# A causal mask carried in unused contraction rows of q and k, in place of identity-triangle products

## The chip, the core and the metric

The kernel runs on one core of a Trainium2 chip. The metric is the device time of one execution in microseconds (us). TensorE (PE in the profile) multiplies, VectorE (DVE) and ScalarE (ACT) read its results, GpSimd (POOL) helps beside them, and every DMA is issued from SyncE's queue (SPq in the profile) and runs on the core's 16 DMA engines.

## What is computed

Sixteen independent batches of 256 tokens of width 128 pass through causal attention with 16 heads of width 8, a residual and a layer norm, then a product with int8-rounded operands, a residual and a second layer norm.

```python
qkv = encodings @ attn_w.T + attn_b            # 16 heads, head width 8
mask = jnp.arange(n)[:, None] <= jnp.arange(n)[None, :]
scores = jnp.einsum('bhki,bhqi->bhkq', k, q) / math.sqrt(HEAD)
scores = jnp.where(mask, scores, NEG_INF)      # key k counts for query q only if k <= q
probs = jax.nn.softmax(scores, axis=2)         # over the keys
combined = jnp.einsum('bhkq,bhkl->bhql', probs, v)
x = _layernorm(x + (combined @ out_w.T + out_b))
x = _layernorm(x + ffn(x))                     # ffn: both operands rounded to int8, product, rescaled
```

## The kernel before

**Scores.** Two heads make a pair (PAIRS = 8). For a pair, 48 contraction rows hold one head and 48 the other: q and k are each split in three bf16 parts, and six products of parts of eight values give 48 rows (ROWS). Rows 96 to 123 are zero, rows 124 to 127 (SHIFT_ROW to DEPTH) carry a shift of each query, its largest score taken off in two bf16 pieces, against ones in `k_stat`. A score tile has 2 x 64 keys (64 of each head, KB = 64) on the partitions and the queries from the first of those keys on as columns: 256, 192, 128 or 64 of them for the four blocks of keys. The triangle on the diagonal is masked by one more product, `identb` by `causal` (-1e30 above the diagonal), which is added to the first 64 columns of every head pair in the bank.

**Units.** The tiles are computed in 12 units for a batch (`UNITS`: first key, first pair, number n of pairs): n is 2 for the first two blocks of keys and 4 for the last two. Every batch goes through the units twice: `scores_for_max` writes to a ring of 3 PSUM banks (`dve_bank`), which DVE reduces to maxima (L642), and `scores_for_exp` to a ring of 4 banks (`act_bank`), which ACT exponentiates into `probs` (L481). The maxima of batch b run 10 units ahead of the exponentials of batch b - 1 or so (`LEAD`): in phase b the exponentials of batch b stand beside the last two units of the maxima of batch b + 1 and the first ten of batch b + 2.

**Phases.** The programs of all engines are a loop over phases b from -4 to 18, each of 12 steps u, one for each unit, with the other work hung in at a fixed step: PE does the products of probabilities and values (`pv`, L860), the projections `project_qk(b + 4)` (L881, at u = 6 and 7), `project_v`, `turn_maxima(b + 1)` (u = 4), the output projection and the feed-forward product of earlier batches. All engines run their own list in order and meet at semaphores.

**From a projection to the scores.** ACT copies q and k of batch b + 4 out of PSUM (L498, L499), POOL, DVE and POOL again split them in three parts (L419, L421, L656, L424). SyncE writes the parts to DRAM images (`write_image`, L302), waits until these have landed, and reads them back into `q_move` and `k_stat`, which form a ring of 4 slots (`read_image`, L315 and L316): four DMAs of 192 KB in pieces of 512 bytes. A phase of SyncE is this list, in this order:

```python
            def phase(b):
                write_image(b + 3, 1)
                load_x(b)
                read_image(b + 3)
                load_xt(b + 5)
                load_shift(b + 1)
                write_image(b + 4, 0)
                store(b - 3)

            phases(phase, {-3: first_rows_stand, -2: next_rows_stand, -1: last_rows_stand})
```

`load_shift(b + 1)` (L325) moves the shift made by DVE (L675) into rows 124 to 127 of `q_move`: two DMAs of 8 KB in pieces of 64 bytes. `scores_for_exp(b + 1, 0)`, the first step of phase b + 1 on PE, waits for them. The `..._rows_stand` functions run before the phases -3, -2 and -1: the second and third copy the ones rows into two slots of `k_stat` each (L337, two DMAs of 32 KB on 4 partitions). POOL sets the constants and clears the buffers before its own phases (L377 to L400).

Of the kernel before, what the change touches and what calls it, by code (L numbers as in the profile page):

```python
# [45 lines left out]
KB = 64  # L46
# [14 lines left out]
MASKED = -1e30  # L61
MAGIC = 12582912.0
# [57 lines left out]
def build_program(nc, x, xt, wqkv_t, bqkv, wo_t, bo, rhs_t, out):  # L120
    ctx = ExitStack()
    with ctx:
# [26 lines left out]
        causal = sb("causal", [128, KB], BF16)  # L149
# [14 lines left out]
        q_move = [sb(f"q_move{i}", [128, PAIRS, TOK], BF16) for i in range(QK_RING)]  # L164
# [42 lines left out]
        ones_loaded = sem("ones_loaded")  # L207
        x_loaded = [sem(f"x_loaded{i}") for i in range(RING)]
# [54 lines left out]
        POOL_FIRST = 14  # L263
        POOL_ROWS = POOL_FIRST + 2 * (QK_RING - 2)
# [6 lines left out]
        def _(sp):  # L271
# [21 lines left out]
            def write_image(b, half):  # L293
# [4 lines left out]
                if half == 0:  # L298
                    wait_ring(sp, qk_loaded, b - QK_RING, 4, 4)
# [5 lines left out]
            def read_image(b):  # L305
# [5 lines left out]
                for s in range(2):  # L311
# [3 lines left out]
                    sp.dma_start(q_move[slot][rows, :, :], q[s]).then_inc(qk_loaded[slot], 16)  # L315
                    sp.dma_start(k_stat[slot][rows, :, s, :], k[s]).then_inc(qk_loaded[slot], 16)  # L316

            def load_shift(b):
# [4 lines left out]
                for part in range(2):  # L323
                    row = SHIFT_ROW + 2 * part
                    sp.dma_start(q_move[b % QK_RING][row:row + 2, :, :].rearrange("s p (c q) -> s (p c) q", q=32),  # L325
                                 shift[:, part, :]).then_inc(shift_loaded, 16)

            def store(b):
# [3 lines left out]
                sp.dma_start(out[b].rearrange("(t p) d -> p t d", p=128), o[:, :, :]).then_inc(stored, 16)  # L332

# [6 lines left out]
            def first_rows_stand():  # L340
                sp.wait_ge(rows_set, 1)
                sp.wait_ge(pool_setup, 1)

            def next_rows_stand():

                sp.wait_ge(rows_set, 2)
                sp.wait_ge(pool_setup, POOL_FIRST)
                set_shift_rows((0, 1))

            def last_rows_stand():  # L350
                sp.wait_ge(pool_setup, POOL_ROWS)
                set_shift_rows(range(2, QK_RING))
# [15 lines left out]
        def _(pool):  # L368
# [8 lines left out]
            step(pool.memset(q_move[0][:, :, :].bitcast(F32), 0.0))  # L377
            step(pool.memset(ident[:, :], 0.0))
            step(pool.memset(identb[:, :], 0.0))
            step(pool.memset(causal[:, :], MASKED))  # L380
# [649 lines left out]
```

## Time and profile before

| | |
|---|---|
| three runs | 284.0, 283.8 and 280.09 us, median 283.8 |
| the profiled execution | 284.06 us, of which the span of its trace is 282.3 |
| busy, share of the span | PE 87%, DVE 69%, ACT 67%, POOL 43% |
| granted TensorE clock, mean | 0.95 |
| DMA | 32.77 MB, 116 GB/s over the span |

A busy share is an average over a start of some 44 us, twelve phases that repeat, four that thin out and a tail; PE's busy time also counts matmuls that wait in the array for one another. What a stage costs is read from the time between the same steps of two phases.

### The profile page before, as it was taken

What the parts mean: (1) busy time and instruction counts of PE and PEld (TensorE: products, weight loads), DVE (VectorE), ACT (ScalarE), POOL (GpSimd) and SP (SyncE); (2) the same over time, 40 slices, a digit from 0 to 9 for tenths busy, and PEclk for the clock granted to TensorE, in tenths of its full rate; (3) what the DMA queues carried; (4) which work ended last, traced back from release to release, by engine and by line L of the source; (5) the groups of instructions that cost most, each with busy time, mean ns of one, the idle gap of its engine ahead of it and who ended that gap; (6) DMA issues with size and microseconds to landing.
All of it is one profiled execution on the core that took longest, in us unless ns stands there. A gap on an engine that the chain in (4) does not pass through costs nothing.

```text
span 282.3 us, 8298 instructions
## 1 busy us (share of the span) xinstructions
PE 244.5 (87%) x3075; PEld 171.2 (61%) x3077; DVE 195.1 (69%) x545; ACT 188.1 (67%) x434; POOL 121.8 (43%) x236
## 2 busy tenths in 40 slices
PE   4179747999999999999999999999999999999420
PEld 2037525676767676767676767676767677565200
DVE  7927853576869696868686868686868797624331
ACT  4202033677687787878787878787878777798341
POOL 7930840041525454545453535353535141532542
PEclk9999985999999999999999999999999999999855
DMA  3385777337554765476547654757466410110001
GB/s 93 111 189 121 165 154 196 77 116 152 173 93 134 133 193 92 151 134 192 91 153 135 192 91 151 135 170 118 151 116 190 76 41 15 31 37 16 7 19 37
DMA packets 50887, 32.77 MB, mean 116 GB/s; under 512 B 7200, under 2 KB 50848, under 8 KB 50848
## 3 DMA queue, kind: packets, MB, share of 16 engines
q1 hardware_dynamic: 50848, 32.26, 47.2%
q8 instruction: 24, 0.39, 0.6%
q14 instruction: 15, 0.12, 0.2%
HBM read 17.17 MB, written 14.68 MB: 113 GB/s over the span
## 4 chain that ended last, share of the span: by engine, by line
PE 81%; DVE 7%; issue 4%; POOL 3%; ACT 3%; DMA 1%; ACTq 0%; SPq 0%; POOLq 0%; DVEq 0%
PE pv_bank L860 18%; PE dve_bank L823 17%; PE act_bank L823 13%; PE act_bank L881 6%; PE dve_bank L826 5%; PE act_bank L826 5%; PE act_bank L891 3%; PE dve_bank L905 3%; PE dve_bank L923 3%; PE pv_bank L960 3%; PE act_bank L914 1%; PE dve_bank L871 1%; PE dve_bank L942 1%; PE act_bank L933 1%; POOL rstd L444 1%
## 5 line engine op out<-in xcount | busy, mean ns | idle before, releaser
L642 DVE TRANSPOSE_TENSOR_REDUCE part_max<-dve_bank 128x16 f32<-128x512 f32 (+1 forms) x192 | 115.8, 615 | 42.7 <-PE dve_bank L826 40.6
L481 ACT ACTIVATE probs<-act_bank 128x512 f32<-128x512 f32 (+1 forms) x192 | 101.2, 530 | 38.0 <-PE act_bank L826 37.1
L823 PE MATMUL act_bank<-q_move,k_stat 128*128 128x128 bf16 (+3 forms) x512 | 68.2, 236 | 6.2 <-issue 6.2
L823 PE MATMUL dve_bank<-q_move,k_stat 124*128 124x128 bf16 (+3 forms) x512 | 71.1, 241 | 1.6 <-DMA k_stat<-imagek 1.3
L860 PE MATMUL pv_bank<-probs,v_stat 128*32 128x256 f32 (+3 forms) x1024 | 61.1, 311 | 0.0
L823 PEld LDWEIGHTS dve_bank<-q_move,k_stat 124*128 124x128 bf16 x512 | 40.3, 117 | 28.9 <-DVE part_max L642 7.5
L419 POOL TENSOR_TENSOR qk_rest<-qk_f,qk_parts 128x512 f32<-128x512 f32 x15 | 17.4, 1162 | 75.5 <-ACT qk_f L499 72.4
L823 PEld LDWEIGHTS act_bank<-q_move,k_stat 128*128 128x128 bf16 x512 | 42.0, 114 | 10.7 <-issue 8.2
L826 PE MATMUL dve_bank<-causal,identb 128*128 128x128 bf16 (+1 forms) x192 | 46.5, 242 | 0.0
L826 PE MATMUL act_bank<-causal,identb 128*128 128x128 bf16 (+1 forms) x192 | 46.0, 240 | 0.0
L498 ACT ACTIVATE qk_parts<-act_bank,bias 128x256 bf16<-128x256 f32 x32 | 21.0, 655 | 26.6 <-PE act_bank L881 24.6
L860 PEld LDWEIGHTS pv_bank<-probs,v_stat 128*32 128x32 f32 x1024 | 20.3, 108 | 19.4 <-issue 9.7
L442 POOL TENSOR_SCALAR rstd<-moments 128x2 f32<-128x2 f32 x32 | 6.1, 191 | 52.7 <-DVE moments L713 35.6
L881 PE MATMUL act_bank<-xt_in,wqkv 128*128 128x256 f32 x64 | 23.3, 455 | 4.2 <-DMA wqkv<-wqkv_dram 3.7
L444 POOL TENSOR_TENSOR rstd<-rstd,minus_half 128x2 f32<-128x2 f32 x32 | 22.4, 699 | 2.7
L424 POOL TENSOR_TENSOR qk_parts<-qk_rest,qk_parts 128x512 bf16<-128x512 f32 x15 | 17.4, 1162 | 10.3 <-DVE qk_parts L656 10.3
L513 ACT ACTIVATE v_stat<-act_bank 64x256 f32<-64x256 f32 x32 | 12.1, 378 | 13.6 <-POOL v_stat L408 7.6
L826 PEld LDWEIGHTS dve_bank<-causal,identb 128*128 128x128 bf16 x192 | 19.0, 99 | 0.3
L826 PEld LDWEIGHTS act_bank<-causal,identb 128*128 128x128 bf16 x192 | 19.1, 99 | 0.1
L499 ACT ACTIVATE qk_f<-act_bank,bias 128x256 f32<-128x256 f32 x32 | 19.1, 596 | 0.0
L881 PEld LDWEIGHTS act_bank<-xt_in,wqkv 128*128 128x128 f32 x64 | 11.0, 205 | 11.4 <-issue 6.0
L565 ACT ACTIVATE o<-r,rstd 128x128 f32<-128x128 f32 x32 | 14.1, 496 | 4.6 <-POOL rstd L448 4.6
(87 smaller groups left out, 319.1 us busy)
## 6 DMA issues: line engine op xcount, KB each, us to landing
imageq<-qk_parts SPq DMA_DIRECT2D x32, 192.0 KB, 2.1
imagek<-qk_parts SPq DMA_DIRECT2D x32, 192.0 KB, 2.1
q_move<-imageq SPq DMA_DIRECT2D x32, 192.0 KB, 3.7
k_stat<-imagek SPq DMA_DIRECT2D x32, 192.0 KB, 4.4
xt_in<-xt_dram SPq DMA_DIRECT2D x16, 128.0 KB, 4.6
x_in<-x_dram SPq DMA_DIRECT2D x16, 128.0 KB, 2.4
out_dram<-o SPq DMA_DIRECT2D x16, 128.0 KB, 2.0
q_move<-shift SPq DMA_DIRECT2D x32, 8.0 KB
```

The source lines that it names most:

```text
L419: pool.tensor_tensor(qk_rest[:, :, :], qk_f[:, :, :], first, ALU.subtract).then_inc(qk_split[1], 1)
L424: pool.tensor_tensor(third, qk_rest[:, :, :], second, ALU.subtract).then_inc(qk_split[1], 1)
L444: pool.tensor_tensor(t[:, 0, :], t[:, 0, :], minus_half[:, :], ALU.pow).then_inc(made[1], 1)
L481: act.activation(probs[u][:, 0:cols], act_bank[at % ACT_BANKS][:, 0:cols], ACT.Exp, scale=SCALE).then_inc(act_emptied, 1)
L498: act.activation(first, src, ACT.Identity, bias=bias[:, w:w + 1])
L499: act.activation(whole, src, ACT.Identity, bias=bias[:, w:w + 1]).then_inc(act_emptied, 1)
L565: act.activation(o[:, t, :], r[:, t, :], ACT.Identity, bias=rstd[1][:, 1, t:t + 1], scale=rstd[1][:, 0, t:t + 1]).then_inc(o_made[1], 1)
L642: dve.tensor_reduce(o32, dve_bank[at % DVE_BANKS][:, 0:n * (TOK - key)].rearrange("k (c q) -> k c q", q=32), op=ALU.max, axis=AX.X, apply_ ...
L823: pe.matmul(tiles[:, j, :], keys, q_move[b % QK_RING][0:rows, p0 + j, key:TOK], start=(j == 0), stop=False, skip_group_check=True)
L826: return pe.matmul(tiles[:, :, 0:KB], identb[:, :], causal[:, :].unsqueeze(1).to_broadcast([128, n, KB]), start=False, stop=True, skip_gro ...
L860: last = pe.matmul(pv_bank[col:col + 32, g, key:TOK], v_stat[b % RING][:, key // KB, p0 + j, :], tiles_of(probs[u], u)[:, j, :], start=(n ...
L881: pe.matmul(bank[:, 0:TOK], wqkv[:, w, :], xt_in[b % XT_RING][:, :], start=True, stop=True).then_inc(act_filled, 1)
```

## The change

The 384 identity products (L826) go. A mask is put into the contraction rows from 96 on, which were zero: row 96 + i belongs to the keys 3i, 3i + 1 and 3i + 2 of a block of 64, so 22 rows do for 64 keys. `k_stat` gets in that row one of three values by the key's place, `q_move` a value by the query's place against the keys of the row, so that the product is a large negative number for a masked pair and zero for others. The mask applies only in the block on the diagonal, so `q_move` now holds two copies of the queries: copy 0 with mask rows (queries 64 to 255 in blocks 1 to 3) and copy 1, in whose mask rows only the first block has the mask. Every score matmul reads block by block from the copy that it needs; for the second block of keys its 192 columns come as two matmuls, of 64 and 128 columns, with the same weights.

```diff
@@ constants @@
+MASK_ROW = 96
+MASK_KEYS = 3
+MASK, MASK_STEP = 2.0 ** 23, 2.0 ** 52
+KEY_VALUES = (1.0 / MASK_STEP, 1.0, MASK_STEP)
+QUERY_VALUES = (-MASK * MASK_STEP, -MASK, -MASK / MASK_STEP)
@@ buffers @@
-        causal = sb("causal", [128, KB], BF16)
+        mask_q = sb("mask_q", [128, 2 * TOK], BF16)
+        mask_k = sb("mask_k", [128, TOK], BF16)
...
-        q_move = [sb(f"q_move{i}", [128, PAIRS, TOK], BF16) for i in range(QK_RING)]
+        q_move = [sb(f"q_move{i}", [128, 2, PAIRS, TOK], BF16) for i in range(QK_RING)]
...
-        POOL_FIRST = 14
-        POOL_ROWS = POOL_FIRST + 2 * (QK_RING - 2)
+        POOL_MASKS = 14
+        POOL_FIRST = 17
+        POOL_ROWS = POOL_FIRST + QK_RING - 2
@@ SyncE: read_image, load_shift @@
-                    sp.dma_start(q_move[slot][rows, :, :], q[s]).then_inc(qk_loaded[slot], 16)
+                    sp.dma_start(q_move[slot][rows, 1, :, :], q[s]).then_inc(qk_loaded[slot], 16)
                     sp.dma_start(k_stat[slot][rows, :, s, :], k[s]).then_inc(qk_loaded[slot], 16)
+                    sp.dma_start(q_move[slot][rows, 0, :, KB:TOK], q[s][:, :, KB:TOK]).then_inc(qk_loaded[slot], 16)
...
-                    sp.dma_start(q_move[b % QK_RING][row:row + 2, :, :].rearrange("s p (c q) -> s (p c) q", q=32),
-                                 shift[:, part, :]).then_inc(shift_loaded, 16)
+                    for copy in range(2):
+                        sp.dma_start(q_move[b % QK_RING][row:row + 2, copy, :, :].rearrange("s p (c q) -> s (p c) q", q=32),
+                                     shift[:, part, :]).then_inc(shift_loaded, 16)
@@ SyncE: rows that stand @@
+            def set_mask_rows(slots):
+
+                for i in slots:
+                    rows = slice(MASK_ROW, SHIFT_ROW)
+                    for copy in range(2):
+                        sp.dma_start(q_move[i][rows, copy, :, :],
+                                     mask_q[rows, copy * TOK:(copy + 1) * TOK].unsqueeze(1).to_broadcast([SHIFT_ROW - MASK_ROW, PAIRS, TOK])).then_inc(mask_loaded[i], 16)
+                    sp.dma_start(k_stat[i][rows, :, :, :].rearrange("r p s q -> r (p s) q"),
+                                 mask_k[rows, :].unsqueeze(1).to_broadcast([SHIFT_ROW - MASK_ROW, 2 * PAIRS, TOK])).then_inc(mask_loaded[i], 16)
...
             def first_rows_stand():
+                sp.wait_ge(pool_setup, POOL_MASKS)
                 sp.wait_ge(rows_set, 1)
-                sp.wait_ge(pool_setup, 1)
+                set_mask_rows((0,))
...
                 sp.wait_ge(pool_setup, POOL_FIRST)
+                set_mask_rows((1,))
                 set_shift_rows((0, 1))
...
                 sp.wait_ge(pool_setup, POOL_ROWS)
+                set_mask_rows(range(2, QK_RING))
                 set_shift_rows(range(2, QK_RING))
@@ POOL: four clears of q_move and the triangle go, six selections and two clears come @@
-            step(pool.memset(q_move[0][:, :, :].bitcast(F32), 0.0))
+            step(pool.memset(mask_q[:, :], 0.0))
+            step(pool.memset(mask_k[:, :], 0.0))
...
-            for half in range(2):
-                m = causal[64 * half:64 * half + 64, :]
-                step(pool.affine_select(out=m, in_=m, compare_op=ALU.is_gt, fill=0.0,
-                                        base=0, pattern=[[-1, KB]], channel_multiplier=1))
+            q_mask = mask_q[:, 0:5 * KB].rearrange("r (n q) -> r n q", q=KB)
+            for after, value in zip((0, 1, 2), QUERY_VALUES):
+                step(pool.affine_select(out=q_mask, in_=q_mask, compare_op=ALU.is_ge if after == 0 else ALU.not_equal,
...
+            k_mask = mask_k[:, :].rearrange("r (k b) -> r k b", b=4)
+            for place, value in enumerate(KEY_VALUES):
+                step(pool.affine_select(out=k_mask, in_=k_mask, compare_op=ALU.not_equal, fill=value,
...
-            step(pool.memset(q_move[1][:, :, :].bitcast(F32), 0.0))
...
-                    step(pool.memset(q_move[i][:, :, :].bitcast(F32), 0.0))
@@ DVE: rhs_scales @@
-                dve.wait_ge(pool_setup, 10)
+                dve.wait_ge(pool_setup, POOL_MASKS)
@@ PE: scores @@
-                    keys = k_stat[b % QK_RING][0:rows, p0 + j, :, :].rearrange("r s (k b) -> r (s k) b", b=4)[:, :, key // KB]
-                    pe.matmul(tiles[:, j, :], keys, q_move[b % QK_RING][0:rows, p0 + j, key:TOK],
-                              start=(j == 0), stop=False, skip_group_check=True)
-
-                return pe.matmul(tiles[:, :, 0:KB], identb[:, :],
-                                 causal[:, :].unsqueeze(1).to_broadcast([128, n, KB]), start=False,
-                                 stop=True, skip_group_check=True)
+                    keys = k_stat[b % QK_RING][0:rows, p0 + j, :, :].rearrange("r s (k b) -> r (s k) b", b=4)[:, :, blk]
+                    queries = q_move[b % QK_RING][0:rows, :, :, :].rearrange("r c p (n q) -> r (c p n) q", q=KB)
+                    masked = 4 * (p0 + j)
+                    plain = 4 * (PAIRS + p0 + j)
+                    if blk == 1:
+                        pe.matmul(tiles[:, j, 0:KB], keys, queries[:, masked + 1, :],
+                                  start=(j == 0), stop=False, skip_group_check=True)
+                        last = pe.matmul(tiles[:, j, KB:3 * KB], keys, queries[:, plain + 2:plain + 4, :],
+                                         start=False, stop=(j == n - 1), skip_group_check=True)
...
@@ PE: scores_for_max @@
                 if u == 0:
-                    wait_ring(pe, qk_loaded, b, 4, 4)
+                    if b < QK_RING:
+                        pe.wait_ge(mask_loaded[b], 48)
+                    wait_ring(pe, qk_loaded, b, 6, 6)
```

## Rows read from the trace of the kernel before

**Rows 1.** Busy time by stretch: nine equal phases, then phases 13 to 15 (us, executed instructions).

```profile
91.88:219.14 127.26, 127.23 (x1715) 91.47 (x1718) 100.07 (x300) 103.52 (x244) 61.77 (x117) 1.00 0.60 144
219.14:232.26 13.12, 13.12 (x190) 9.41 (x194) 10.96 (x34) 9.83 (x24) 3.97 (x10) 1.00 0.32 59
232.26:244.76 12.50, 12.18 (x179) 8.43 (x182) 9.39 (x30) 9.51 (x23) 3.97 (x10) 1.00 0.10 24
244.76:254.34 9.58, 9.02 (x127) 5.60 (x130) 3.45 (x17) 8.67 (x22) 3.93 (x10) 1.00 0.12 31
```

**Rows 2.** Waits of ACT and DVE in the nine phases (total us, times, longest).

```profile
ACT probs L481 <- PE act_bank L826: 14.2, 27, 0.8
...
DVE part_max L642 <- PE dve_bank L826: 19.0, 27, 1.0
```

**Rows 3.** The chain of waits at the end of the start.

```profile
38.14 6.15 issue
44.29 0.59 PE act_bank L823 x2
```

**Rows 4.** Timeline of POOL and SyncE's queue in the start.

```profile
5.19 1.38 POOL L392 TENSOR_SCALAR_AFFINE_SELECT shift_on<-shift_on 128x512 bf16<-128x512 bf16 x2
...
14.27 0.32 SPq L315 DMA_DIRECT2D q_move<-imageq  x1
...
25.11 0.32 SPq L315 DMA_DIRECT2D q_move<-imageq  x1
...
30.82 1.34 SPq L337 DMA_DIRECT2D k_stat<-shift_on  x2
...
37.03 0.32 SPq L315 DMA_DIRECT2D q_move<-imageq  x1
...
39.45 1.16 SPq L325 DMA_DIRECT2D q_move<-shift  x2
```

**Rows 5.** Timeline of PE in phase 8 (start, us, line, operands).

```profile
152.39 0.22 PE L826 MATMUL dve_bank<-causal,identb 128*128 128x128 bf16 x1
152.45 0.33 PE L823 MATMUL act_bank<-q_move,k_stat 128*128 128x192 bf16 x2
152.61 0.22 PE L826 MATMUL act_bank<-causal,identb 128*128 128x128 bf16 x1
...
155.24 0.29 PE L823 MATMUL act_bank<-q_move,k_stat 128*128 128x64 bf16 x4
155.36 0.27 PE L826 MATMUL act_bank<-causal,identb 128*128 128x256 bf16 x1
155.47 0.61 PE L923 MATMUL dve_bank<-wo,heads_d 128*128 128x128 f32 x4
```

**Rows 6.** DMA engines from 32 to 36 us, in 40 slices of 0.1.

```profile
DMA  0122022123257999852332223123041697997333
GB/s 0 31 31 31 10 31 20 20 36 31 26 108 241 276 312 266 241 82 41 56 41 41 26 26 36 10 20 31 0 41 10 210 323 261 358 317 272 123 123 138
```

**Rows 7.** Timeline, all engines, from 126 to 157 us: one batch's way to its scores.

```profile
128.20 0.38 PE L823 MATMUL act_bank<-q_move,k_stat 128*128 128x256 bf16 x2
...
137.49 0.70 PE L881 MATMUL act_bank<-xt_in,wqkv 128*128 128x256 f32 x2
...
143.72 0.47 SPq L302 DMA_DIRECT2D imagek<-qk_parts  x1
...
147.22 0.32 SPq L315 DMA_DIRECT2D q_move<-imageq  x1
...
149.98 1.12 SPq L325 DMA_DIRECT2D q_move<-shift  x2
...
156.47 0.38 PE L823 MATMUL act_bank<-q_move,k_stat 128*128 128x256 bf16 x2
```

**Rows 8.** DMA engines from 148 to 154 us, in 40 slices of 0.15.

```profile
DMA  2356699999999999999999999999976546111000
GB/s 55 102 123 143 201 300 328 297 297 198 143 147 137 212 143 137 140 140 150 178 256 283 242 242 256 277 236 260 197 146 98 91 64 148 30 29 9 9 3 0
```

More of the change, by code:

```diff
@@ L207, in build_program @@
         ones_loaded = sem("ones_loaded")
+        mask_loaded = [sem(f"mask_loaded{i}") for i in range(QK_RING)]
         x_loaded = [sem(f"x_loaded{i}") for i in range(RING)]
@@ L298, in write_image @@
                 if half == 0:
-                    wait_ring(sp, qk_loaded, b - QK_RING, 4, 4)
+                    wait_ring(sp, qk_loaded, b - QK_RING, 6, 6)
                 for w in range(2):
@@ L385, in _ @@
                                         base=0, pattern=[[-1, 128]], channel_multiplier=1))
-            for half in range(2):
-                m = causal[64 * half:64 * half + 64, :]
-                step(pool.affine_select(out=m, in_=m, compare_op=ALU.is_gt, fill=0.0,
-                                        base=0, pattern=[[-1, KB]], channel_multiplier=1))
+            q_mask = mask_q[:, 0:5 * KB].rearrange("r (n q) -> r n q", q=KB)
+            for after, value in zip((0, 1, 2), QUERY_VALUES):
+                step(pool.affine_select(out=q_mask, in_=q_mask, compare_op=ALU.is_ge if after == 0 else ALU.not_equal,
+                                        fill=value, base=MASK_KEYS * MASK_ROW - max(after - 1, 0),
+                                        pattern=[[0, 5], [1, KB]], channel_multiplier=-MASK_KEYS))
+            k_mask = mask_k[:, :].rearrange("r (k b) -> r k b", b=4)
+            for place, value in enumerate(KEY_VALUES):
+                step(pool.affine_select(out=k_mask, in_=k_mask, compare_op=ALU.not_equal, fill=value,
+                                        base=MASK_KEYS * MASK_ROW - place, pattern=[[1, KB], [0, 4]],
+                                        channel_multiplier=-MASK_KEYS))
             step(pool.memset(shift_on[:, :, :], 0.0))
@@ L670, in make_shift @@
                     if b > 0:
-                        dve.wait_ge(shift_loaded, 32 * b)
+                        dve.wait_ge(shift_loaded, 64 * b)
                     dve.tensor_copy(shift[:, 0, :], turned[:, 64:96]).then_inc(shift_made[1], 1)
@@ L819, in scores @@
                 key, p0, n = UNITS[u]
+                blk = key // KB
                 tiles = tiles_of(bank, u)
                 for j in range(n):
-                    keys = k_stat[b % QK_RING][0:rows, p0 + j, :, :].rearrange("r s (k b) -> r (s k) b", b=4)[:, :, key // KB]
-                    pe.matmul(tiles[:, j, :], keys, q_move[b % QK_RING][0:rows, p0 + j, key:TOK],
-                              start=(j == 0), stop=False, skip_group_check=True)
-                return pe.matmul(tiles[:, :, 0:KB], identb[:, :],
-                                 causal[:, :].unsqueeze(1).to_broadcast([128, n, KB]), start=False,
-                                 stop=True, skip_group_check=True)
+                    keys = k_stat[b % QK_RING][0:rows, p0 + j, :, :].rearrange("r s (k b) -> r (s k) b", b=4)[:, :, blk]
[7 more added lines that the diff above has]
+                                         start=False, stop=(j == n - 1), skip_group_check=True)
+                    else:
+                        if blk == 0:
+                            blocks = queries[:, plain:plain + 4, :]
+                        elif blk == 2:
+                            blocks = queries[:, masked + 2:plain + 4:plain + 1 - masked, :]
+                        else:
+                            blocks = queries[:, masked + 3:masked + 4, :]
+                        last = pe.matmul(tiles[:, j, :], keys, blocks,
+                                         start=(j == 0), stop=(j == n - 1), skip_group_check=True)
+                return last
             def scores_for_max(b, u):
@@ L842, in scores_for_exp @@
                         pe.wait_ge(ones_loaded, 16 * QK_RING)
-                    pe.wait_ge(shift_loaded, 32 * (b + 1))
+                    pe.wait_ge(shift_loaded, 64 * (b + 1))
                 scores(b, u, act_ring(("exp", b, u)), DEPTH).then_inc(act_filled, 1)
```

1 line of the change is left out of this document (removed).

## The prediction

> **What bounds the kernel now.** I read first where the time lies, by stretches [rows 1]. From 91.88 to 219.14 us nine phases take 14.14 us each, and PE is busy in all of it; DVE is busy 100.07 / 9 = 11.1 us of a phase and ACT 103.52 / 9 = 11.5. The waits [rows 2] agree: DVE and ACT wait for scores (19.0 and 14.2 us in nine phases), while PE has no wait there. So in the middle PE's own work is the time. In front stands a start: the chain of waits has PE idle for 6.15 us until 44.29 [rows 3], when the first product for exponentials begins, which needs the first shift. SyncE's queue [rows 4] shows the way there: the images of batches 0, 1 and 2 are read at 14.27, 25.11 and 37.03, then comes the first shift at 39.45. Behind that is a tail of four thinner phases [rows 1] and the drain.
>
> **The products that go.** A triangle of 128 columns holds PE for 0.06 us (152.39 to 152.45), one of 256 for 0.11 (155.36 to 155.47) [rows 5]; the 0.22 and 0.27 printed as durations are passages through the array and overlap. A phase has 16 of the first and 8 of the second: 0.96 + 0.88 = 1.84 us. The split of 192 columns comes back: two of 192 take 0.16 us, 0.08 each, against 0.03 for 64 (four in 0.12) and 0.055 for 128 [rows 5], so 0.005 for each of 16, and 0.08 in all. PE's work falls by 1.76 to 12.38 us a phase. ACT at 11.5 and DVE at 11.1 fit under that; their waits of 2.1 and 1.6 us a phase in [rows 2] would shrink to about 0.5, and I would add 0.2 for their uneven steps if nothing else came in the way.
>
> **The transfers of a batch.** Something does come, and it can be seen in one batch's way [rows 7]. Phase 6 starts at 128.20; its second projection, of batch 10, runs at 137.49 (9.29 later); the last image write is issued at 143.72 (6.23); the images are read from 147.22 (3.50); behind these reads SyncE issues the shift of batch 8 at 149.98, and phase 8 starts at 156.47. The DMA engines [rows 8] are full from about 148.9 to 152.5 and end the shift at about 153.7. The first packets appear 1.0 us after the issue; I take as much for the landing, an estimate: 154.7. So the shift is there only 1.7 us before its phase, and of the 28.27 us from phase 6 to phase 8 all but that is a chain in which only the first 9.29 is PE's work. PE must not get much faster, and the change lengthens the rest of the chain:
> - Two reads for copy 0, 2 x 144 KB. The four reads, 768 KB in 1536 pieces, take about 4.0 us in [rows 8]. By bytes the new ones take 1.5 us, by pieces (768 of 384 bytes) 2.0. Their issue, 0.5 each, is hidden, for the queue is the later one. I take 1.5, as the rate in [rows 8] moves between 140 and 300 GB/s with pieces of one size.
> - Two more shift DMAs. Two issue in 1.12 us [rows 7], and the thin tail of [rows 8] is about 1.1 us long. So 0.6 (part hidden) to 1.1; I take 1.0.
>
> Together 2.5 us (1.8 to 3.1). Against it the 9.29 shrinks by the triangles before the second projection, 12 x 0.06 + 4 x 0.11 - 0.05 = 1.1. From phase 6 to phase 8: 28.27 - 1.7 + 2.5 - 1.1 = 28.0 us, so 14.0 a phase, against 14.14. The loop closes on every second batch, so one parity sets the pace for both. The 1.76 us that PE saves turn into idle time at the start of a phase. Over phases 2 to 12 that leaves 5 x 0.3 = 1.5 us, less 0.3 for the first ones, which have the longer read and no margin: -1.2 (0 to -6).
>
> The copies behind it: `read_image`'s wait for the exponentials of four batches ago keeps its cover, and the maxima of a batch start several us after its reads, so a read 1.5 us later moves nothing there.
>
> **The start.** SyncE now issues three mask DMAs for slot 0 ahead of the second half of image 0, three for slot 1 ahead of that of image 1, six for slots 2 and 3 ahead of that of image 2. Everything for the first shift queues behind them. A slot takes 28 partitions x (8 + 8 + 16) x 512 bytes = 448 KB. Not shown before, so from both sides: at the 200 GB/s or so of [rows 8], 2.1 us a slot. But the ones rows, the one transfer of this kind (from and to the same few partitions, spread by a broadcast), crawl: two DMAs of 32 KB, issued at 30.82 [rows 4], keep the engines at 10 to 40 GB/s from 32.0 to 35.5 [rows 6]. That is 16 KB a partition in 3.4 us, and a slot's mask is 16 KB a partition too: 3.4 us. I take 3.2, near this row, as it is the same kind. Four slots: 12.8 us (8.4 to 13.6). Reads of copy 0 for three batches ahead of the shift: 4.5 us (3.9 to 6). The shift: 1.0. Slack that absorbs some: the queue stands idle for about a microsecond between the reads and the next image in places, -0.8. First product for exponentials 17.5 us later, at about 61.8 (low 11.8, high 20.5).
>
> The Trainium skill bears on this twice. "SBUF — State Buffer", section on the DMA port swizzle, has partitions 96 to 127 behind half of the 16 DMA ports; "DMA: Bandwidth & Descriptors", on why a DMA increments its semaphore by 16, would run a transfer over 28 partitions on 14 engines. By either the masks cost more than bytes over the full rate, as the slow rows of [rows 6] suggest; no run here shows the ports themselves.
>
> POOL's setup: two clears and six selections before POOL_MASKS, where DVE's first step now waits. A selection over 512 columns takes 0.69 us (two in 1.38) [rows 4], these have 320 and 256. Some 3 us more on POOL, four clears less; DVE's start moves by 0 to 0.5 us, against transfers that are 12 us longer. I count nothing.
>
> **The end.** Without projections the chain is gone and PE is the bound again: -1.75 each for two phases, -1.1 for that with exponentials and two units of maxima (12.50 us [rows 1]), and of the last one's 0.9 I take 0.4, as ACT is busy 8.67 of 9.58 there [rows 1]. In all -5.0.
>
> **Sum.** Against the profiled execution's 284.06 us (span 282.3): + 17.5 - 1.2 - 5.0 = 295.4, so 295 us. The median of three runs is 283.8, a quarter of a microsecond from it, so nothing is scaled.
>
> **Rivals.**
> 1. The transfers are cheap: masks at the full rate (start + 11.8) and 1.8 us in the chain, so 27.3 for two phases, -5. 284.06 + 11.8 - 5 - 5 = 286 us. For it: masks write 28 partitions, not 4. Against: [rows 6]. Chance 0.21.
> 2. The other side, faster: the chain gives way and PE sets the pace. It does if what lies between projection and shift shrinks by itself when PE idles, because ACT, DVE and POOL then reach their steps sooner. It decides from the point where the added transfers cost less than 24.8 - 25.5 = -0.7 us, that is, where they are hidden and the chain is shorter by 0.7 besides. Then 12 phases gain 1.7: 284.06 + 11.8 - 20.4 - 5 = 270.5 us; half of it gives 277. Against: the steps from 137.49 to 147.22 follow one another with no queueing that I can see. Chance 0.08.
> 3. The pieces of 384 bytes are slow, or the clock falls. If each piece takes as much as two of 512 bytes would, the chain gets 2.5 us more, two phases take 30.5, and the start 7 more: some 310 us. "DMA: Bandwidth & Descriptors" in the Trainium skill has transfers under 512 bytes as read-modify-write; [rows 8] has only 512 and 64 byte pieces and does not decide. Or the idle 3 us before every second phase lower the granted clock, as the 6.15 us did at 38.14 [rows 3] (the pair of products after it takes 0.59 us, the same pair 0.38 in [rows 7]); a few us each time would give the same 310. Chance 0.09.
> 4. The masks cost what I say and the change doesn't do what it says on PE, since the split or the strided reads take back the gain: the chain hides that too, 297 us. It is inside my case.
>
> **How the numbers follow.** My case 0.62, rival 1 0.21, rival 2 0.08, rival 3 0.09. The range leaves out rivals 2 and 3 and goes from the low end of rival 1 (283) to the high end of mine, 284.06 + 20.5 + 0 - 4.5 = 300, with 4 more for a chain at 3.1: 304. Two per cent, 5.7 us, is what a measurement of this kernel can tell from no change. Faster 0.08, same 0.22, slower 0.70.
>
> **What would show it.** The first `act_bank` product near 61.8 instead of 44.29; masks at low GB/s with a third to half of the engines' time; phases in the middle near 14.0 us with PE idle 1.5 us or more in each, before the first product for exponentials, and `load_shift` ending just before it. Wrong in the middle: PE busy throughout and phases of 12.5 us. Wrong in the start: mask DMAs that finish in 2 us a slot. ACT or DVE without waits would mean a bound that I have not priced.

## The result, and the profile after

The changed kernel takes 298.01 us (median of four runs, 296.69 to 299.54) against 283.86 us for the kernel before beside it (280.09 to 284.0): a ratio of 1.0534 (of the means, as all ratios below), with a 95% interval of 1.0431 to 1.0638. It is slower. The profiled execution took 298.71 us, with a span of 297.1.

The first lines of its page:

```profile
span 297.1 us, 8127 instructions
PE 229.4 (77%) x2949; PEld 153.1 (52%) x2949; DVE 194.1 (65%) x545; ACT 185.4 (62%) x434; POOL 122.5 (41%) x237
PE 31%; SPq 14%; POOL 12%; DVE 12%; DMA 11%; issue 11%; ACT 8%; ACTq 0%; POOLq 0%; DVEq 0%
```

PE is busy for 77% of the span where it was busy for 87%, and in the third line, the shares of the chain that ended last, SyncE's queue, the DMA engines and "issue" (time in which an engine waited for nothing that the profile shows) have 36%. Now the busy times by stretch: phases 3 to 11, then phases 12, 13 and 14, then the rest. The columns, here and in [rows 1], are the stretch and its length, the busy time (and number of instructions) of PE, of PE's weight loads, DVE, ACT and POOL, then the granted clock, the busy share of the DMA engines and what they moved in GB/s:

```profile
101.44:227.75 126.31, 117.67 (x1642) 81.20 (x1640) 99.62 (x298) 101.40 (x242) 61.65 (x117) 0.99 0.69 164
227.75:242.90 15.15, 12.06 (x182) 8.19 (x179) 12.69 (x39) 10.51 (x27) 6.21 (x14) 1.00 0.65 153
242.90:254.90 12.00, 11.74 (x178) 8.17 (x179) 9.37 (x27) 9.26 (x22) 2.89 (x7) 1.00 0.08 17
254.90:264.94 10.04, 9.41 (x145) 5.88 (x144) 5.34 (x23) 8.75 (x22) 3.96 (x10) 1.00 0.13 31
264.94:297.10 32.16, 14.16 (x164) 8.11 (x162) 11.65 (x52) 16.96 (x43) 13.05 (x34) 0.72 0.09 25
```

I measure every kernel below by the start of the first product for exponentials of each batch: of batch 0 (the start), from batch 3 to batch 12 (the mean phase), and from batch 12 to the end of the span (the tail). Before: 44.29, 14.14 and 69.3 us. After: 61.09, 14.03 and 69.35. The span grew by 14.8 us: the start is 16.8 longer, the twelve phases from batch 0 to batch 12 give back 2.1 (1.0 of it from batch 3 on), and the tail is the same. The phases of [rows 1] are cut at another step of the same program, so single phases of before are given below by the step used here.

**The middle.** PE is idle for 8.64 us of these nine phases, 0.96 a phase, where it had no idle time [rows 1]. Waits of PE from 101 to 228 us (total, times, longest):

```profile
PE act_bank L871 <- DMA q_move<-shift: 5.6, 4, 1.9
PE dve_bank L860 <- DVE part_max L674: 2.5, 14, 0.2
```

All of PE's long waits are the four of the first line, for the shift. The timeline of one loop, from phase 5 to phase 7, answers to [rows 7] line by line:

```profile
129.06 0.41 PE L871 MATMUL act_bank<-q_move,k_stat 128*128 128x256 bf16 x2 [0.81 <-DMA q_move<-shift]
...
137.75 0.70 PE L928 MATMUL act_bank<-xt_in,wqkv 128*128 128x256 f32 x2
...
144.00 0.46 SPq L315 DMA_DIRECT2D imagek<-qk_parts  x1
...
147.53 0.32 SPq L328 DMA_DIRECT2D q_move<-imageq  x1
...
151.04 3.93 SPq L340 DMA_DIRECT2D q_move<-shift  x4
...
156.65 0.41 PE L871 MATMUL act_bank<-q_move,k_stat 128*128 128x256 bf16 x2 [1.08 <-DMA q_move<-shift]
```

From the phase to the second projection it is 8.69 us (9.29 before), to the last image write 6.25 (6.23), to the reads 3.53 (3.50), and from the first read to the phase after next 9.12 (9.25). At the start of phases 5, 7, 9 and 11 PE stands still until the shift has landed, 0.81 to 1.91 us, so that the phase in front of each takes 14.3 to 15.4 us. Phases 5, 7 and 9 themselves, which no such wait ends, take 13.02 to 13.03. The two lengths make the mean. DMA engines, 150 to 157 us in slices of 0.175:

```profile
DMA  9999999999999999999999956111011011119999
GB/s 165 168 168 161 147 130 123 133 151 150 166 164 187 255 307 316 303 302 303 304 293 288 214 96 130 18 18 16 9 18 18 8 18 18 11 61 395 421 369 395
```

The engines are full with the reads until 154.1 us. Then come the four small shift transfers, some 2 us at 8 to 18 GB/s and a tenth of the engines.

The shift is not the only thing that holds PE. DVE's waits in the same stretch, and below them a line of the kernel before, from 91.88 to 219.14 us:

```profile
DVE qk_parts L688 <- POOL qk_parts L453: 9.7, 10, 1.0
```

```profile
DVE qk_parts L656 <- POOL qk_parts L421: 6.6, 9, 0.7
```

In every phase DVE stands at its part of the split of q and k until POOL is ready, 0.7 us a phase before the change and 1.0 after it. The experiments show what that costs.

The last of the nine phases, 11, has no wait for the shift at its end and yet took 14.35 us. The granted clock, the third column from the right, tells why:

```profile
184.97:198.00 13.03, 12.78 (x183) 8.94 (x183) 9.18 (x29) 10.39 (x24) 5.69 (x12) 1.00 0.68 154
213.40:227.75 14.35, 14.09 (x182) 9.61 (x183) 9.21 (x27) 10.38 (x24) 5.69 (x12) 0.88 0.61 138
214.22:217.63 3.41, 3.41 (x48) 2.24 (x44) 1.36 (x3) 1.64 (x4) 1.29 (x4) 0.50 0.65 208
```

With the same work as phase 9, phase 11 had a granted clock of 0.88: for 3.41 us, just behind the wait of 1.91 us at 213.40, the lower level of 1.2 GHz was granted. PE lost 1.3 us by it (14.35 against 13.03). Behind the start, the clock had fallen in the same way once before, at 87.92, behind the wait of 2.54 us at 87.44. It did not fall after the waits of 1.81 us at 184.97 and 2.69 us at 242.90.

**The start.** SyncE's queue before the first phase:

```profile
13.19 0.33 SPq L315 DMA_DIRECT2D imageq<-qk_parts  x1
...
14.12 1.94 SPq L354 DMA_DIRECT2D q_move<-mask_q  x2
16.09 0.81 SPq L356 DMA_DIRECT2D k_stat<-mask_k  x1
...
21.32 0.32 SPq L328 DMA_DIRECT2D q_move<-imageq  x1
...
34.95 0.32 SPq L328 DMA_DIRECT2D q_move<-imageq  x1
...
51.72 0.32 SPq L328 DMA_DIRECT2D q_move<-imageq  x1
...
55.17 3.87 SPq L340 DMA_DIRECT2D q_move<-shift  x4
```

The first reads of the three images stand at 21.32, 34.95 and 51.72, where they stood at 14.27, 25.11 and 37.03 [rows 4]: 7.1, 9.8 and 14.7 us later. The first image write is late already, at 13.19 (10.78 before, an unshown line of the same view). POOL's and DVE's timelines say why:

```profile
5.54 2.88 POOL L421 TENSOR_SCALAR_AFFINE_SELECT mask_k<-mask_k 128x256 bf16<-128x256 bf16 x3
```

```profile
8.53 0.56 DVE L645 TENSOR_SCALAR bv_all<-ones,bias 128x128 f32<-128x128 f32 x1 [2.85 <-issue]
```

DVE's first step waits for POOL_MASKS and stands for 2.85 us, until the selections are done at 8.42.

The DMA engines from 44.5 to 47.5 us, in slices of 0.075, with the masks of the last slots in flight:

```profile
DMA  9898889888979788878988988997878989788765
GB/s 355 150 150 137 144 157 157 143 130 157 150 130 150 130 150 143 130 137 150 150 137 137 164 137 150 150 157 123 143 123 150 164 150 171 137 143 137 123 96 109
```

The masks do not crawl as the ones rows of [rows 6] did, at 10 to 40 GB/s and 0.1 to 0.3 of the engines' time. They run at some 145 GB/s with the engines busy for 0.8 to 0.9 of the time. At that rate the 448 KB of a slot take 3.1 us.

### The profile page after: what moved, and what is told of

The parts are those of the page before. It is cut to its first block, busy times and chain, and to the rows that moved or that the text cites. A ratio compares the mean times of both kernels' runs of the same rounds, so it can differ in the third digit from the quotient of the medians.

```text
span 297.1 us, 8127 instructions
## 1 busy us (share of the span) xinstructions
PE 229.4 (77%) x2949; PEld 153.1 (52%) x2949; DVE 194.1 (65%) x545; ACT 185.4 (62%) x434; POOL 122.5 (41%) x237
## 4 chain that ended last, share of the span: by engine, by line
PE 31%; SPq 14%; POOL 12%; DVE 12%; DMA 11%; issue 11%; ACT 8%; ACTq 0%; POOLq 0%; DVEq 0%
PE pv_bank L907 9%; SPq L340 6%; DVE part_max L674 5%; PE act_bank L871 5%; DMA q_move<-shift 4%; PE dve_bank L871 4%; ACT qk_f L531 3%; DMA imagek<-qk_parts 3%; POOL qk_rest L451 3%; PE act_bank L928 3%; PE dve_bank L952 3%; ACT qk_parts L530 2%; DVE ffn L772 2%; PE act_bank L938 2%; DMA k_stat<-shift_on 2%
## 5 line engine op out<-in xcount | busy, mean ns | idle before, releaser
L871 PE MATMUL act_bank<-q_move,k_stat 128*128 128x128 bf16 (+2 forms) x384 | 47.8, 234 | 21.8 <-issue 10.9
L871 PE MATMUL dve_bank<-q_move,k_stat 124*128 124x128 bf16 (+2 forms) x384 | 50.1, 241 | 9.3 <-DMA q_move<-imageq 9.3
L871 PEld LDWEIGHTS dve_bank<-q_move,k_stat 124*128 124x128 bf16 x384 | 30.3, 118 | 28.7 <-issue 14.0
L871 PEld LDWEIGHTS act_bank<-q_move,k_stat 128*128 128x128 bf16 x384 | 26.7, 117 | 25.6 <-issue 12.8
L860 PE MATMUL dve_bank<-q_move,k_stat 124*128 124x64 bf16 x128 | 20.1, 208 | 3.4 <-DVE part_max L674 3.3
L862 PE MATMUL dve_bank<-q_move,k_stat 124*128 124x128 bf16 x128 | 20.7, 229 | 0.0
L862 PE MATMUL act_bank<-q_move,k_stat 128*128 128x128 bf16 x128 | 20.2, 225 | 0.0
L860 PEld LDWEIGHTS dve_bank<-q_move,k_stat 124*128 124x128 bf16 x128 | 12.1, 117 | 13.5 <-DVE part_max L674 11.7
L860 PE MATMUL act_bank<-q_move,k_stat 128*128 128x64 bf16 x128 | 18.5, 196 | 0.0
L688 DVE CAST qk_parts<-qk_rest 128x512 bf16<-128x512 f32 x16 | 8.4, 524 | 14.3 <-POOL qk_parts L453 14.3
```

Of the source, the lines that this page charges most:

```text
L860: pe.matmul(tiles[:, j, 0:KB], keys, queries[:, masked + 1, :], start=(j == 0), stop=False, skip_group_check=True)
L862: last = pe.matmul(tiles[:, j, KB:3 * KB], keys, queries[:, plain + 2:plain + 4, :], start=False, stop=(j == n - 1), skip_group_check=True)
L871: last = pe.matmul(tiles[:, j, :], keys, blocks, start=(j == 0), stop=(j == n - 1), skip_group_check=True)
```

## The experiments

Two questions. In the middle: is the loop of transfers the bound, with PE's saving spent in waiting for the shift, or do the new products not save what was counted, or another engine hold them? In front: the mask transfers, or something else that the change put there?

**Old products, new transfers.** The products of before with the triangle, beside all the transfers, the masks and both copies of the changed kernel. It masks by both.

```diff
-                    queries = q_move[b % QK_RING][0:rows, :, :, :].rearrange("r c p (n q) -> r (c p n) q", q=KB)
...
+                    pe.matmul(tiles[:, j, :], keys, q_move[b % QK_RING][0:rows, 1, p0 + j, key:TOK],
+                              start=(j == 0), stop=False, skip_group_check=True)
+
+                return pe.matmul(tiles[:, :, 0:KB], identb[:, :],
+                                 causal[:, :].unsqueeze(1).to_broadcast([128, n, KB]), start=False,
+                                 stop=True, skip_group_check=True)
```

> The changed kernel with the identity-triangle products of before put back (scores read copy 1 only, one matmul a pair, then the triangle); all transfers and mask rows of the change stay. PE has 1.76 us more to do in a phase than in the changed kernel. If the transfers set the pace (my reading), only the 1.1 us ahead of the second projection enters the loop of two phases: the start stays as in the changed kernel (first product for exponentials near 61 us), phases of about 14.5 us, total about 304 us. If the changed kernel's phases of 14.0 us are set by the engines' own work, PE's 1.76 come on top of each: phases near 15.8, total about 319. If the changed products are what cost the time, this kernel is as fast as before plus the start: 301 us with phases of 14.14.

304.09 us, a ratio of 1.0747 (1.0677 to 1.0818). Start 59.86, phase 14.48, tail 69.55. The phase is 0.34 us longer than that of the kernel before, with the same products: what the transfers add. Two phases of 15.20 and 15.33 us hold most of it; the others took 14.16 to 14.53, so PE is nearly the bound again. It is 0.45 longer than that of the changed kernel: what the products are worth while the loop holds. By the prediction's loop, 28.0 + 1.1 us for two phases, it would be 14.55. PE's work alone would have made the second difference 1.76.

**One copy.** No reads of copy 0 and no shift for it; all matmuls read copy 1. The masks of keys 64 to 255 are left out.

```diff
-                    sp.dma_start(q_move[slot][rows, 0, :, KB:TOK], q[s][:, :, KB:TOK]).then_inc(qk_loaded[slot], 16)
...
-                    for copy in range(2):
+                    for copy in (1,):
```

> The changed kernel without the reads of copy 0 and without its shift rows: four reads and two shift DMAs a batch, as before; the masked blocks read copy 1 too, so the mask of keys 64 to 255 is left out. PE's instructions and the mask rows of the start stay. If the added transfers stretch the loop from projection to shift: the start ends 4 to 5.5 us earlier (near 56 us), and the loop falls by 2.3 to 2.5 us for two phases, until the engines are the bound; phases 6 and 8 of the changed kernel, which had no wait for the shift, took 13.0, so 13.0 a phase, total about 282 us. If instead DVE or ACT set the 14.0, the phases stay and the total is about 292 us.

281.95 us, 0.9984 (0.9947 to 1.0021). Start 56.43, phase 13.33 (expected 13.0), tail 66.35. PE's products are the same in number and size as after, so the copy costs 0.70 us a phase, 4.7 in the start and 3.0 in the tail. But 13.33 is not the 12.6 that PE alone would give. From 93 to 213 us (nine phases) its waits list:

```profile
DVE qk_parts L687 <- POOL qk_parts L452: 9.9, 10, 1.0
...
PEld dve_bank L859 <- DVE part_max L673: 9.3, 27, 0.4
```

DVE reaches its part of the split of q and k (the cast at L687) a microsecond before POOL is ready, and stands there in every phase. Behind it stand its maxima, and PE's weight loads wait for the banks that these would free. That would be a second loop: projection, ACT, POOL, DVE's cast, the maxima behind it, PE. The runs with the projection earlier put it to the test.

**Copy behind the shift.** The same transfers as after; only their order in SyncE's queue differs.

```diff
                 load_shift(b + 1)
+                read_copy(b + 3)
                 write_image(b + 4, 0)
```

> The changed kernel with one thing moved: SyncE issues the two reads of copy 0 after the shift's DMAs instead of ahead of them. Same bytes, same number of DMAs. If it is the place in the queue that costs, the shift lands 1.5 to 2 us earlier, the maxima's scores have room for the later read: phases of 13.1 to 13.3 us, the start 1.5 us shorter, total about 287 us. If it is the load on the DMA engines as such, nothing moves: 298 us.

288.87 us, 1.0198 (1.0139 to 1.0256). Start 61.21, phase 13.44, tail 67.53. With every byte kept, the phase falls by 0.59 us of the 0.70 that the copy costs. So in the middle it is what stands ahead of the shift in the queue that costs, not the traffic. From the first read to the shift's last packet it is now 7.0 us (mean of four loops that end in a shift wait after, single ones within 0.4), where the changed kernel has 8.6 and the kernel before 6.2: the copy ahead of the shift costs 1.6 us a loop, the two more shift DMAs 0.8. The start, expected 1.5 us shorter, did not move: the copies of batches 0 and 1 still stand ahead of the masks, and the third image is read at 53.11, 1.4 us later than after.

**Projection earlier.** The changed kernel, with `project_qk(b + 4)` at steps 4 and 5 in place of 6 and 7, and ACT's reads of it too.

```diff
-                    if u == 6:
+                    if u == 4:
                         qk_from_psum(b + 4, 0)
-                    if u == 7:
+                    if u == 5:
                         qk_from_psum(b + 4, 1)
```

> The changed kernel with the projections of q and k for batch b + 4 two steps earlier in a phase, at u = 4 and 5 (on PE, on ACT and in the ring of banks). No byte and no instruction more or less. If the loop from projection over the images to the shift sets the pace, it gets some 2.2 us longer a start for two phases: phases fall from 14.0 to 12.9 to 13.1 us, total 286 to 289 us. If the load on the DMA engines or PE's own work sets it, the phases stay at 14.0 and the total at 298.

282.81 us, 0.9992 (0.9966 to 1.0018). Start 60.81, phase 12.93, tail 66.13. No transfer is touched and 1.1 us a phase come back, so that the total is 3 us under the least that was expected. Both loops got shorter by the move: DVE no longer stands at the cast, and with the products of the changed kernel the phases that no shift wait ends take 12.51 to 12.53 us (13.02 after). The others take 12.8 to 13.9, as PE still waits for the shift, for instance at 124.63:

```profile
124.63 0.41 PE L871 MATMUL act_bank<-q_move,k_stat 128*128 128x256 bf16 x2 [0.72 <-DMA q_move<-shift]
```

**Maxima unmasked.** The kernel before, with the triangle taken only from the products for maxima. These then include keys after the query; the shift is an upper bound, and it cancels in the softmax.

```diff
+                if rows == SHIFT_ROW:
+                    return last
                 return pe.matmul(tiles[:, :, 0:KB], identb[:, :],
```

> The kernel before, with the triangles left out of the scores for the maxima alone; the exponentials keep theirs. The shift is then the maximum over a query's whole blocks of keys and no longer of the allowed keys; it cancels in the softmax. No transfer changes. PE has 0.92 us less a phase. If PE's work is the time of the kernel before and its loop of transfers has the 1.7 us of room that I read from its trace (two phases: 28.27 - 1.7 - 0.56 = 26.0): phases of 13.2 to 13.3 us, total 272 to 274 us. If the loop has no such room, or DVE sets the pace at once: 14 us a phase and 282 us.

271.96 us, 0.9612 (0.9567 to 0.9656). Start 42.93, phase 13.43, tail 67.83. Half of the triangles gives 0.71 us a phase.

**Maxima unmasked, projection earlier.** Both edits.

> The kernel before with the maxima unmasked, and the projections two steps earlier. Without the move the phases were 13.43 us where PE's work is 13.22. If PE waits because DVE waits for POOL's split of the projection (1.0 us a phase in the run with one copy loaded), that goes: 13.2 us a phase, total 269 to 270 us. If DVE's own work is the bound, nothing moves: 272 us.

267.88 us, 0.9452 (0.9403 to 0.9502). Start 43.12, phase 13.09, tail 67.87. The move gives 0.34 us a phase more.

**No mask transfers.** The mask is left out altogether: rows 96 to 127 of `q_move` are set to zero by four ACT instructions of 3.5 us in place of the mask DMAs. POOL's selections, DVE's wait, the copy and its shift stay.

```diff
-                        sp.dma_start(q_move[i][rows, copy, :, :],
-                                     mask_q[rows, copy * TOK:(copy + 1) * TOK].unsqueeze(1).to_broadcast([SHIFT_ROW - MASK_ROW, PAIRS, TOK])).then_inc(mask_loaded[i], 16)
...
+                    act.activation(q_move[i][96:128, :, :, :].rearrange("r c p q -> r (c p q)"),
+                                   warm[96:128, 0:1].to_broadcast([32, 2 * PAIRS * TOK]), ACT.Copy).then_inc(rows_zeroed, 1)
```

> The changed kernel without the twelve mask transfers of the start; rows 96 to 127 of both copies are set to zero by ACT, so the mask is left out altogether. POOL's setup, the copies and the shifts stay. From the trace of the changed kernel the masks cost 4.6 us before image 0, some 1.4 before image 1 and 3.4 before image 2: the first product for exponentials near 51.6 us instead of 61.1, phases as there (14.0), total near 289 us. If the start is late by POOL's setup and the copies and not by the masks, it stays near 59 to 61 us and the total near 297.

284.51 us, 1.0062 (1.0039 to 1.0085). Start 47.47 (expected 51.6), phase 13.74, tail 69.93. Its timeline:

```profile
47.47 0.59 PE L873 MATMUL act_bank<-q_move,k_stat 128*128 128x256 bf16 x2 [4.55 <-issue]
```

The start falls from 61.09 to 47.47: the masks cost 13.6 us, 3.4 a slot on average. The first reads of the three images come at 16.55, 27.47 and 38.08, so the first slot's masks had cost 4.8 us, the second's 2.7 and the last two 6.2 together. The remaining 3.2 over the kernel before are 2.4 for the late image write (13.22) and 0.8 for copy reads and shift.

**Setup wait short.** DVE waits for POOL's step 8, the last that it needs, and not for POOL_MASKS.

```diff
-                dve.wait_ge(pool_setup, POOL_MASKS)
+                dve.wait_ge(pool_setup, 8)
```

> The changed kernel, with DVE's first step waiting for POOL's ones and identities (8 steps) instead of all mask selections (14). The run without mask transfers still read image 0 at 16.55 us, 2.3 later than before. If that is POOL's setup holding up DVE, the images of batch 0 are written near 10.8 to 11.2 us instead of 13.2, and the first product for exponentials comes up to 2.3 us earlier, 58.8 to 59.5 instead of 61.1; total about 296 us. If the clears of k_stat on POOL hold DVE up anyway, or the mask transfers take up the slack, it stays at 61.

294.25 us, 1.0431 (1.0367 to 1.0496). Start 57.27 (expected 58.8 to 59.5), phase 14.06, tail 68.66. SyncE's queue and PE:

```profile
9.57 0.33 SPq L315 DMA_DIRECT2D imageq<-qk_parts  x1
```

```profile
57.27 0.59 PE L871 MATMUL act_bank<-q_move,k_stat 128*128 128x256 bf16 x2 [11.06 <-issue]
```

The image write moves by 3.62 us and the first phase by 3.82. The wait was on the path in full, and nothing behind it had slack. It is 2.4 of the change's cost; the other 1.2 to 1.4 the kernel before had too, for its own wait was for step 10.

**One copy, partial rows.** A kernel that keeps the mask rows for the exponentials and needs no copy. The shift has rows 96 to 99, the mask rows 100 to 121. A product on the diagonal contracts over all rows, one to the right of it over rows 0 to 99 alone. The maxima are unmasked and contract over 96. ACT writes the mask and ones rows of all slots from two small tiles, so no DMA does.

```diff
-SHIFT_ROW = 124
-DEPTH = SHIFT_ROW + 4
...
-MASK_ROW = 96
+SHIFT_ROW = 96
+DEPTH = 128
+MASK_ROW = 100
...
+                    last = pe.matmul(tiles[:, j, 0:KB], keys, queries[:, key:key + KB],
+                                     start=(j == 0), stop=(key == 3 * KB and j == n - 1), skip_group_check=True)
+                    if key < 3 * KB:
+                        last = pe.matmul(tiles[:, j, KB:TOK - key], keys[0:MASK_ROW], queries[0:MASK_ROW, key + KB:TOK],
+                                         start=False, stop=(j == n - 1), skip_group_check=True)
```

> The mask in contraction rows without a second copy and without a transfer more: rows 96 to 99 are the shift, 100 to 121 the mask; the block on the diagonal is a matmul of 64 columns over all rows, the other blocks one over rows 0 to 99; the scores for the maxima take rows 0 to 95 and have no mask (the shift cancels in the softmax). ACT fills the constant rows, so the slow ones-row transfers go too. The start should end near 40 us (44.3 before), and as the loop of transfers has its old length, the engines' own loop is the bound, 13.3 us as with one copy loaded: total 265 to 268 us. If the 24 more matmuls a phase cost more than 10 ns each, up to 270. If the loop of transfers binds after all, phases near 14 and 274.

266.76 us, 0.942 (0.9393 to 0.9446). Start 41.05, phase 13.35, tail 66.49. The phase is that of the one copy, 13.33: the second loop, now without the first.

**Partial rows, projection earlier.** The same with the projection at steps 4 and 5.

> The kernel with one copy and partial rows (266.8 us), with the projections at u = 4 and 5 as in the run that moved them. Its phases were 13.35 us with DVE waiting 1.0 us a phase for POOL's split; with the move that wait should go, and PE's own work of about 12.5 is left: phases of 12.5 to 12.7 us, total 257 to 259 us. If the loop of transfers or DVE binds, phases near 13 and 263.

260.7 us, 0.9237 (0.9205 to 0.927), the fastest of all, 7.6% under the kernel before. Start 40.96, phase 12.57, tail 66.19. Busy times from batch 3 to batch 12:

```profile
76.72:189.82 113.10, 113.10 (x1714) 84.58 (x1712) 100.55 (x298) 102.95 (x243) 61.90 (x118) 1.00 0.57 158
```

PE is busy in all of it, and nine phases of 12.57 us follow one another without any difference. DVE's wait for POOL's part of the split is gone from the trace with the move, and the phase fell by 0.78 us (13.35 to 12.57): the second loop is shown. Without it and without the added transfers, this form of the mask is worth 1.57 us a phase.

## Why the prediction was right, and where it was not

**Phases in the middle, 14.0: the number right (14.03), the mechanism right in part.** The loop from phase to phase of one parity holds PE. With copy reads and second shift gone it opens (13.33), with the copy reads behind the shift it opens (13.44), and with the projection earlier it shortens (12.93). The run with the old products (14.48) says less, since PE is nearly the bound there. The terms by the loop shown: "together 2.5 us" measured 2.0, as the way from the first read to the shift's last packet was 6.5 us (147.2 to 153.75) and became 8.5 (147.5 to 156.07). The mean of four loops is 2.4, 1.6 of it for the copy (my 1.5) and 0.8 for the shift (my 1.0). The slack, for which I took 1.7, was 2.1: the last packet is 0.6 us ahead of PE at 156.65, not my 1.0. The 9.29 shrank by 0.6, not by 1.1. So this loop takes 27.6 us for my 28.0. The later ones take 28.3 and 28.4, for their step from the last image write to the reads grew from 3.5 to 4.0 and 4.1 us, and the clock took 1.3 us in phase 11. Neither was in the prediction, and without them the mean would lie near 13.8, an estimate from the loops of 27.6 us: that it came out at 14.03 is in part luck. Why the step to the reads grows, no run settles.

PE's saving is also not all spent in waiting for the shift, as I had it. "PE idle 1.5 us or more in each" phase did not come: PE is idle for 0.96 us a phase, of which 0.6 is the shift. Phases 5, 7 and 9 take 13.02 where the same products take 12.53 with the projection earlier. That fits the second loop, of which the prediction knows nothing. A sign of it was in the trace: DVE's wait for POOL's part of the split, 6.6 us in nine phases of the kernel before, is not among [rows 2].

**"PE's work falls to 12.38, and I would add 0.2": right.** The same products took 12.51 to 12.53 us in the phases of the run with the projection earlier that no shift wait ends, and the partial rows 12.57. With the transfers gone but the projection in its old place the phases stop at 13.33 and 13.35. So rival 2, "the chain gives way and PE sets the pace", could not have come to 12 phases less 1.7 us by itself.

**The start, 61.8: the sum near (61.09), two terms off.** The masks, "3.2, near this row": 13.6 us in all for my 12.8. The number is right and the reason for it wrong. I took it from the ones rows [rows 6], as transfers of the same kind, and named "masks at low GB/s with a third to half of the engines' time" as the sign. The masks ran at some 145 GB/s with 0.8 to 0.9 of the engines' time; that is near the lower of the two rates in [rows 8] and gives 3.1 us by bytes. That the slow row came to nearly the same price is luck. Rival 1, 2.1 us a slot, falls even so. "DVE's start moves by 0 to 0.5 us ... I count nothing" failed: 2.4 us. The cover that I named, transfers that are 12 us longer, was no cover, for DVE's split of batch 0 comes ahead of them on one chain and the two add. And the selections with a stride of four elements took 0.96 us each for 256 columns, more than those over 512. "Reads of copy 0 ... 4.5" and the shift's 1.0, less 0.8 of slack, were too much when the masks are out (0.8 together), right beside them (4.7 by the one-copy kernel). They have no price of their own: what they cost depends on what queues beside them. With 13.6 + 2.4 + 0.8 = 16.8 the sum closes in one order of removal; the other order gives the copies more and the masks less, and I can't say which is theirs.

**The end, -5.0: wrong, 0.** This is the largest miss of the sum. The failed step is "without projections the chain is gone and PE is the bound again". The last reads are those of batch 15, and they still stand ahead of a shift. SyncE's queue and PE, phase 12:

```profile
233.79 0.32 SPq L328 DMA_DIRECT2D q_move<-imageq  x1
...
236.78 3.88 SPq L340 DMA_DIRECT2D q_move<-shift  x4
...
242.90 0.41 PE L871 MATMUL act_bank<-q_move,k_stat 128*128 128x256 bf16 x2 [2.69 <-DMA q_move<-shift]
```

So phase 12 took 15.15 us for my 11.4 (13.13 before). Its loop began at 213.40, and the low clock of phase 11 had made the last projection 1.3 us late, so about half of the 2.69 us of waiting is the clock's, an estimate. Phase 13, with as many products as phase 12, took 12.00 (13.13 before), a gain of 1.1 for my 1.75, though PE was busy for 11.74 of it. Phase 14 took 10.04 (10.58 before), 0.5 for my 1.1, and the rest gained 0.3 for my 0.4. The three phases together come to +0.3 where I had -4.6. With the projection earlier the tail is 66.13, 3.2 shorter: most of the gain was there, held by one read and in part by the clock.

**The total.** 295 was forecast and 298.01 measured (298.71 in the profiled execution). The misses partly cancel: 5.0 us too little for the end, against 0.7 too much for the start and 0.9 for the middle, where phases 0 and 1, which the prediction counts at nothing, gave back 1.3 us.

**Rival 3** falls with its size of 310 us, but half of what it names took place. The new pieces of 384 bytes did not make the chain 2.5 us longer still: two phases took 27.6 to 28.4 us, not 30.5. Two rows of the page, size and median us from issue to landing:

```profile
q_move<-imageq SPq DMA_DIRECT2D x32, 192.0 KB, 3.9
...
q_move<-imageq SPq DMA_DIRECT2D x32, 144.0 KB, 4.4
```

The 144 KB reads stand behind the others in the queue, and the slices above hold 300 GB/s with them in flight. The granted clock did fall behind waits for the shift, as the rival has it, but only twice after the start (87.92 and 214.22) and not before every second phase. The second of these cost the 1.3 us above. The first pair after the idle start took 0.59 us, as before.

## What to carry to other kernels

When one engine is the bound, take each batch's whole way round, with every queue that it shares, and compare its length with that of the phases it spans before you remove work from the engine: the slack was some 2 us in 28 and the added transfers used it up, so a saving of 1.76 a phase was worth 0.1. Look for a second such way as well: here it held PE at 13.0 to 13.3 us a phase. Small transfers that something waits for belong ahead of large ones in a queue, and the work that begins the long way round belongs as early in the phase as its inputs allow; the second cost no byte and gave the changed kernel 1.1 us a phase. (On the kernel before alone it was not run.) A wait on the setup of another engine should name the last step that it needs.

## What the runs showed of the hardware

- Two DMAs that spread a few partitions by a broadcast ran at very different rates: the masks, from and to 28 partitions, at some 145 GB/s with 0.8 to 0.9 of the engines' time (44.5 to 47.5 us), the ones rows, 4 partitions, at 10 to 40 GB/s with 0.1 to 0.3 of it [rows 6]. Both come to some 3.4 us for 16 KB a partition, the masks as a mean of 13.6 us for four slots. A rule by bytes a partition is not shown by these two.
- The same rows written by ACT cost less than by DMA. In the run with partial rows and the projection earlier, four instructions over 32 partitions x 4096 elements took 14.12 us and four of 2048 elements 7.30, beside SyncE's queue and not in it, and the first phase began at 40.96.
- SyncE's issue of a small DMA is not a fixed 0.5 us. Four shift DMAs took 3.93 us to issue behind full reads: 0.52, 1.20, 1.56 and 0.52. At 248.85 and 260.32, with no reads ahead, the same four took 2.20. Two took 1.1 us behind the reads of the kernel before. What is issued behind such a DMA starts later by that.
- The lower granted clock came 0.8 and 0.5 us behind waits of PE of 1.9 and 2.5 us (213.40 and 87.44), stayed for 3.4 us each time, and made a phase of 13.03 us one of 14.35. It did not come after waits of 1.8 and 2.7 us (184.97 and 242.90).
